# Loading the slot tiles by four transfers of 32 strided partitions instead of three of contiguous ones

## The reference, cut to what matters

```
in_agg  = segment_sum(edge_feat, dst, num_segments=6250)
out_agg = segment_sum(edge_feat, src, num_segments=6250)
h   = relu(concat([in_agg, out_agg, x], axis=1) @ W1 + b1)
out = layernorm(x + h @ W2 + b2)
```

## Time and profile before

| | |
|---|---|
| median of 3 runs | 1498.37 us (1495.05 to 1502.81) |
| the profiled execution's own time | 1498.98 us |
| its span, first to last instruction | 1497.2 us |
| busy: PE, PEld, DVE, ACT, POOL | 80%, 68%, 84%, 68%, 68% of the span |
| bytes moved by DMA | 270.44 MB, 181 GB/s over the span |

### The profile page before, as it was taken

The page is one execution under the profiler, slowest core; times in us unless marked ns, Lnnn a source line. Parts: engine busy times, 40 slices in busy tenths (PEclk is TensorE's granted clock), DMA queues, the critical chain, the costliest instruction groups (busy, mean ns, idle before and its releaser), DMA issues.

```text
span 1497.2 us, 65347 instructions
## 1 busy us (share of the span) xinstructions
PE 1200.7 (80%) x23743; PEld 1022.0 (68%) x23743; DVE 1253.8 (84%) x3739; ACT 1016.1 (68%) x2315; POOL 1011.9 (68%) x615
## 2 busy tenths in 40 slices
PE   3667588888989889888888787777778787777797
PEld 2636477777878778778777676576677676666643
DVE  6665799999999999999999787777778886777776
ACT  6334599899999999999888655445556564555443
POOL 4878888888888888888888774463364445435423
PEclk9977799999999999999999989998999999999998
DMA  8332599999999999999999998987898979778731
GB/s 292 31 39 17 92 214 218 204 217 215 219 217 211 217 216 215 218 213 222 240 237 238 214 169 169 190 171 156 173 201 188 198 169 191 169 159 168 164 117 58
DMA packets 260280, 270.44 MB, mean 181 GB/s; under 512 B 97907, under 2 KB 221396, under 8 KB 259926
## 3 DMA queue, kind: packets, MB, share of 16 engines
q1 hardware_dynamic: 174504, 240.40, 59.0%
q0 software_dynamic: 85472, 27.20, 24.0%
q10 hardware_dynamic: 144, 0.60, 0.1%
HBM read 151.35 MB, written 116.75 MB: 179 GB/s over the span
## 4 chain that ended last, share of the span: by engine, by line
PE 29%; issue 24%; DMA 23%; POOL 15%; DVE 6%; ACT 1%; SPq 1%; POOLq 1%; DVEq 0%; ACTq 0%
PE psum L1680 20%; DMA out_tables<-payload,target 18%; POOL out_tables L756 14%; DMA slots_in<-slot_tiles 3%; DVE to_node L1309 2%; PE psum L1852 1%; PE psum L1843 1%; DVE same L1336 1%; PE psum L1632 1%; PE psum L1702 1%; PE psum L1639 1%; PE psum L1656 1%; PE psum L1864 1%; PE psum L1595 1%; PE psum L1720 1%
## 5 line engine op out<-in xcount | busy, mean ns | idle before, releaser
L756 POOL DMA_INDIRECT out_tables<-payload,target x580 | 978.5, 1687 | 410.0 <-DVE target L1317 199.5
L1656 PE MATMUL psum<-parts,to_slot 128*128 128x194 bf16 x5084 | 489.4, 248 | 29.7 <-ACT slots_out L851 25.0
L1680 PE MATMUL psum<-to_node,slots_in 64*64 64x286 bf16 x10824 | 392.3, 299 | 108.2 <-issue 98.7
L1656 PEld LDWEIGHTS psum<-parts,to_slot 128*128 128x128 bf16 x5084 | 422.6, 98 | 62.7 <-ACT slots_out L851 48.8
L1680 PEld LDWEIGHTS psum<-to_node,slots_in 64*64 64x64 bf16 x10824 | 346.6, 113 | 147.9 <-issue 110.0
L851 ACT ACTIVATE slots_out<-psum 128x388 bf16<-128x388 f32 x984 | 406.6, 474 | 54.0 <-PE psum L1656 39.6
L1270 DVE TENSOR_SCALAR to_slot<-iota_h,slot 128x640 bf16<-128x640 f16 (+1 forms) x984 | 344.7, 397 | 17.6 <-PE psum L1656 14.4
L1309 DVE TENSOR_SCALAR to_node<-iota_h,slot_rel 128x286 bf16<-128x286 f16 x902 | 252.8, 303 | 7.2 <-PE psum L1680 5.0
L917 ACT ACTIVATE to_node<-apart 128x286 bf16<-128x286 bf16 x300 | 126.2, 436 | 143.6 <-PE psum L1680 142.9
L1309 DVE TENSOR_SCALAR to_node<-iota_rows,slot_rel 128x286 bf16<-128x286 f16 x602 | 207.6, 345 | 0.0
L909 ACT ACTIVATE apart<-iota_h,slot_rel 128x286 bf16<-128x286 f16 x300 | 143.6, 522 | 24.4 <-DVE slot_rel L1281 24.3
(11 more groups left out here) (137 smaller groups left out, 977.2 us busy)
## 6 DMA issues: line engine op xcount, KB each, us to landing
slot_tiles<-slots_out SPq DMA_DIRECT2D x164, 388.0 KB
feat<-in_edge_attr SPq DMA_DIRECT2D x195, 256.0 KB
slots_in<-slot_tiles SPq DMA_DIRECT2D x42, 763.9 KB
slots_in<-slot_tiles SPq DMA_DIRECT2D x42, 727.5 KB
slot_tiles<-slots_out SPq DMA_DIRECT2D x82, 291.0 KB
slots_in<-slot_tiles SPq DMA_DIRECT2D x84, 127.3 KB
slots_in<-slot_tiles SPq DMA_DIRECT2D x84, 121.2 KB
out_tables<-payload,target POOLq DMA_INDIRECT x580
```

Source lines behind the costliest of these rows:

```text
L756: e.indirect_dma_start(out_tab, at, payload[b][:, t, :], None, element_offset=k * TABLE_ROWS * D, compute_op=ALU.add).then_inc(s_tab[k], 16)
L1656: last = e.matmul(ps_share[r % BANKS][:, o:o + SLOT_W], to_slot[m][:, COLUMN_FROM[k] + t * P:COLUMN_FROM[k] + (t + 1) * P], parts[b][:, SH ...
L1680: return e.matmul(ps_groups[g % 2][h][cols, 0:HOT], slots_in[p % RING][rows, j - PART_FROM[p], D * k:D * (k + 1)], to_node[rows, node_buf( ...
```

## The change

The number of rows, the bytes, the order of the parts and all waits stay. What changes is into how many transfers a part's 128 rows are cut, and which partitions each of them fills. Before, one transfer brings the 96 home rows into partitions 16 to 111, and two bring 16 shared rows each into partitions 0 to 15 and 112 to 127. After, three transfers (`j` = 0, 1, 2) bring the home rows of two of the six columns each, 32 rows, into partitions `j`, `j + 4`, `j + 8` and so on, and a fourth brings the 32 shared rows into partitions 3, 7, 11 and so on. The 32 shared rows of a pair lie behind each other in HBM, so that they are one transfer. The first sixteen rows of each transfer are the first group's and fall into partitions below 64, as they must.

```
-LOADS = 3
+LOADS = MINI // 2 + 1
+assert 2 * SHARED == 4 * HOMES[0] == P // LOADS
...
-                both = 2 * HOMES[0]
-                e.dma_start(into[SHARED:P - SHARED, :], homes[both * g:both * (g + 1), :, a * SLOT_W:z * SLOT_W]
+                both, shared = 2 * HOMES[0], 2 * SHARED
+                for j in range(LOADS - 1):
+                    e.dma_start(into[j:P:LOADS, :], homes[both * g:both * (g + 1), 2 * j:2 * j + 2, a * SLOT_W:z * SLOT_W]
+                                ).then_inc(s_slot_in[p % RING], 16)
+                at = HOME_AT[MINI] + shared * g
+                e.dma_start(into[LOADS - 1:P:LOADS, :], slot_rows[at:at + shared, a * SLOT_W:z * SLOT_W]
                             ).then_inc(s_slot_in[p % RING], 16)
-                for h in range(2):
-                    at = HOME_AT[MINI] + SHARED * (2 * g + h)
-                    e.dma_start(into[(P - SHARED) * h:(P - SHARED) * h + SHARED, :], slot_rows[at:at + SHARED, a * SLOT_W:z * SLOT_W]
-                                ).then_inc(s_slot_in[p % RING], 16)
```

## The result

| | before | after |
|---|---|---|
| median of 4 runs each | 1497.89 us | 1425.53 us |
| ratio | | 0.9502, 95% interval 0.9457 to 0.9546 |
| span of the profiled execution | 1497.2 us | 1425.4 us |

The account below looks back on a forecast made before the run. PE, with its code gaps, was taken to set the slot-load stage, loads binding only at some places. Gains of 4, 2 and 0.5 us sum to 6.5, from 1498.98 to 1492.5 (1492 for the median); 8-in-10 range 1479 to 1511.

Parts of the forecast that it names:

- term 1: Load loop in the slot-load stage: earlier landings gain 4 us over seven places in the chain, capped at 22.9 us.
- Issue: SP's four issues of some 0.57 us each send a part's last transfer about 0.6 us later; landing cost taken as 0.2.
- Landing: Each part's slot load lands 0.8 us earlier, with bounds of 2.8 us earlier and 0.6 us later.
- term 2: PE's 47 code-fetch gaps: code packets come sooner if rows leave sooner, 0.05 us each (0 to 0.65), 2 us together.
- Term 3: The eight early load pieces at 700 to 850 us, where DMA engines are full, gain 0.5 us.
- The signs: In the slot-load stage, DVE's load wait falls from 83.6 to 50 to 60 us; PE's issue gaps stay near 100 us.
- The large gain: Rival: two small transfers slow each slot load, which lands 1.6 to 2.8 us earlier; 1477 us (1474 to 1489), chance 0.25.
- Four transfers cost more than three: Rival: per-transfer cost or strided partitions make slot loads land, say, 1.5 us later; 1531 us (1506 to 1531), chance 0.20.

Follow-up runs that it names:

- e6_later: Changed kernel with SP's wait before each load raised by four tiles, so loads are issued later: 1434.64 us, ratio 0.9522 to the first kernel.
- e11_before_later: First kernel with SP's wait before each load raised by four tiles: 1545.86 us, ratio 0.9978 to the unedited first kernel.
- e3_five: Changed kernel with its fourth transfer cut into two of 16 rows, each into every fourth partition of one half: 1432.94 us, ratio 0.9497.
- e1_block32: Changed kernel's four transfers of 32 rows put into blocks of 32 neighbouring partitions instead of every fourth: 1482.56 us, ratio 0.9853 to the first kernel.
- e9_shape: Changed kernel's load made one transfer of 128 neighbouring HBM rows, walked as 16 times 8 (wrong sums): 1560.31 us, ratio 1.0069 to the first kernel.
- e2_one128: Changed kernel's load made one transfer of 128 rows in a row into 128 partitions (wrong rows): 1418.55 us, ratio 0.9400 to the first kernel.
- e10_half: Changed kernel loading half the bytes of each part from the second pair of groups on (wrong sums): 1504.30 us, ratio 0.9696 to the first kernel.
- e10_again2: Changed kernel with half the bytes in each load from the second pair on, run again on another chip: 1519.92 us, ratio 0.9770.
- e12_two64: Changed kernel's load made two transfers of 64 rows, each into every second partition, shared slots renumbered: 1526.73 us, ratio 0.988 to the first kernel.
- e4_two: Changed kernel's load made two transfers, 96 rows into partitions 0 to 95 and 32 into 96 to 127: 1537.67 us, ratio 0.984, slower chip.
- after_fourth: Changed kernel unedited, run again as a partner on a slower chip: 1520.97 us, ratio 0.975 to the first kernel.
- after_again: Changed kernel unedited, run again as a partner on a slower chip: 1510.58 us, ratio 0.973 to the first kernel.

## Why the prediction was wrong

**The reading of the stage was right as far as it went.** (The stage itself is a little longer than the 860 to 1410 us that stand ahead of the prediction: 847.5 to 1417.2.) PE and not DVE sets it, DVE's waits for loads are mostly covered by PE's code gaps (e6_later, e11_before_later), and the part of the gain that comes by the load loop is small: the wait for one-hots fell by 2.5 us (23.6 to 21.1), where term 1 said 4.

**Issue.** The median of the four issues is 0.59 us (0.57 was said), but the second takes 1.45 us in the load shown above, and the last issue ends 3.3 us after the first began. The landing came earlier all the same.

**Landing.** Forecast 0.8 us earlier, measured about 1.5 in the two loads compared. Inside the bounds and, by e6_later, without much effect.

**The step that failed is term 2**, "the code gaps ... between 0 and 0.65 us for each of 47 gaps. Since bytes and rows stay, I take 0.05, or 2 us". At PE they lost 44.2 us, about 1 us a gap, outside even the bound of 0.65. Two things are wrong in that step. First, the bound priced the code packet's own duration alone, and that fell by only 0.16 us (1.23 to 1.07). The other 0.8 us of a gap has no term in the prediction. That it is time which the packet spends waiting behind rows on its engine is theory K; it is likely and not shown. Second, "bytes and rows stay" was taken as a reason for no change, when what changed is for how long a row holds its engine: 15.0 against 18.7 GB/s per busy engine. The rows for it were in the profile: the sharing chunks move 204 GB/s and more with the engines full, 13 GB/s an engine in rows of 776 B and 2 KB, and the stage of the loads makes no more than 15.0 of rows up to ten times as long. The prediction made this comparison (178 against 214 to 240 GB/s) but used it for the landing alone.

**A term that was missing: PE's clock.** 24.6 us of busy time went with the clock's rise from 0.93 to 0.98. The granted clock in that stage and what follows a gap of nearly 4 us could have been seen in the stretches shown above. I never asked what a gap costs beyond its own length.

**Term 3**, 0.5 us in the sharing chunks: the stage before the loads ended 1.8 us later, no gain.

**The signs.** The prediction called itself wrong if the code gaps shrink along with DVE's waits, "then they were no code gaps, or depend on the loads". Both shrank. That they are code gaps is not withdrawn, since after the change runs of 122 and 123 weight loads stand between them too, half of the 246 of the earlier trace rows:

```profile
1017.54 3.69 PEld L1681 LDWEIGHTS psum<-to_node,slots_in 64*64 64x64 bf16 x123 [1.71 <-issue]
1022.48 3.71 PEld L1681 LDWEIGHTS psum<-to_node,slots_in 64*64 64x64 bf16 x122 [1.24 <-issue]
```

That they depend on the loads is what the runs show. DVE's wait fell to 31.5 us, below the 50 to 60 that were named.

**The rivals.** The large gain came nearest. It named the narrow transfers as the cause, which is half right: rows in neighbouring partitions are slow, 16 rows as such are not (e3_five). With it stood the rule of the Trainium skill ("SBUF — State Buffer", section on the DMA port swizzle); the runs agree with that rule as far as partitions go: e1_block32 gives up seven tenths of the gain, at 15.1 GB/s. They don't agree where all 128 partitions are reached with a 16 by 8 walk, at 14.5 GB/s (e9_shape). And the rival's price, 22 us, missed as the forecast did: 15 us for one-hots, where 2.5 were measured, and 0.1 to 0.2 us a code gap, where it was 1. "Four transfers cost more than three" did not happen: e3_five has five at the same time. The other rule of the Trainium skill that was quoted for it ("SBUF — State Buffer", summary of rules: one transfer and not several) is right for e2_one128 and wrong for the single transfer of 16 by 8 rows, which is the slowest of all.

**What is shown and what is argued.** Shown by runs: that the partitions matter at equal count, size and source (e1_block32), that the landing does not (e6_later, e11_before_later), that bytes do not once the rows are spread (e10_half and e10_again2, on slower chips only), that the walk of the source matters at equal rows and partitions (e9_shape), and the order of four, two and one (e12_two64 with its group). Read from the traces: that the gain sits in the issue gaps and the clock. Argued: why neighbouring partitions are slow (that their rows wait for each other), and that the code packets wait behind slot rows (K). Both tests of K missed in time, so it stands on the lengths of the gaps and on the exclusion of L alone. Argued too is how rows are given to the DMA engines (S), against which stand e4_two and the untested order of the reads in HBM. A part of S would fit the Trainium skill ("DMA: Bandwidth & Descriptors", the section on the descriptor swizzle), by which in a plain transfer of 128 partitions each engine writes one port of its own: e2_one128 has the highest rate of all. The 16 by 8 walk would then be a shape of 128 partitions that does not get it; no trace here shows which engine writes which partition.

## What to carry to other kernels

When transfers share the DMA engines with instruction fetch, ask for how long each row holds its engine (MB over share times engines times time), not only when the load lands; the rate per busy engine put nine kernels here in nearly the right order. It does not tell all: e1_block32 and the first kernel have 15.1 and 15.0 and lie 1.5% apart. Into which partitions a transfer goes, and in which order its source is walked, can move that rate from 14 to 21 GB/s with the same bytes: try one transfer whose both sides are 128 plain rows (here it was only possible with the wrong rows), then pieces that stride over all partitions, and measure a source of several dimensions before trusting it. And price PE's gaps with the clock that they lose.

## What the runs showed of the hardware that was not expected

**The walk of the source.** 128 partitions from 128 rows in a row: 0.940 on a chip like the first and 0.954 on a slower one. The same rows walked 16 by 8: 1.007 on a slower one. No count, no size and no set of addresses explains that; the order of the addresses might.

**Chips differ in a way that hides part of the gain.** On the four chips where the first kernel took 1540 to 1562 us, PE pauses by up to 0.6 us within tile products, about every 1.9 us where it is densest, with nothing to wait for. The changed kernel on such a chip (after_fourth), weight loads:

```profile
1100.06 1.16 PEld L1681 LDWEIGHTS psum<-to_node,slots_in 64*64 64x64 bf16 x36 [0.60 <-issue]
1101.84 1.36 PEld L1681 LDWEIGHTS psum<-to_node,slots_in 64*64 64x64 bf16 x45 [0.61 <-issue]
1103.77 1.03 PEld L1681 LDWEIGHTS psum<-to_node,slots_in 64*64 64x64 bf16 x34 [0.58 <-issue]
```

On the first chip a run of 246 weight loads has no such pause. The granted clock of this run in 950 to 1350 us is 1.00 nevertheless. The pauses are most frequent where the long gaps are gone. Of PE's gaps of "issue" in the stage, on one and the same chip, the first kernel with later loads (e11_before_later) has 46.5 us in gaps of 0.8 us or more and 10.5 us in 28 gaps of 0.2 to 0.8 us; the changed kernel (after_again) has 5.8 and, in 114 of the shorter ones, 41.9. So most of what the change takes from the long gaps comes back in short pauses, and it brings 2.5% instead of 5%. What makes the pauses was not found.
